# A graph layer on one core: who clears the accumulator, and when the statistics of the raw rows are taken

## The reference

```python
h = relu(layernorm(x))
s, v = h[:, :64], h[:, 64:].reshape(n, 32, 3)
xs = s @ W1_s / sqrt(64);  xv = einsum('nmc,mk->nkc', v, W1_v) / sqrt(32)     # per node: the "table"
w  = silu(edge_embed @ fc_w1 + fc_b1) @ fc_w2 + fc_b2                         # per edge, 192 weights
xs_e, xv_e = xs[src], xv[src]                                                 # gathered by source
m0_a = w_ss * xs_e * sh0;          m1_a = (w_sv * xs_e)[:, :, None] * sh1[:, None, :]
m1_b = w_vs[:, :, None] * xv_e * sh0;  m0_b = w_vv * einsum('emc,ec->em', xv_e, sh1) / sqrt(3)
agg  = segment_sum(concat(m0_a, m0_b, m1_a, m1_b), dst) / sqrt(0.5)
out_s = agg_s @ W2_s / sqrt(96) + s @ Wsc_s / 8
out_v = einsum(agg_v, W2_v) / sqrt(96) + einsum(v, Wsc_v) / sqrt(32)
return x + h + concat(silu(out_s[:, :64]), out_v * silu(out_s[:, 64:96])[:, :, None])
```

## Time and profile before

| | |
|---|---|
| median of 3 runs | 535.98 us (534.12 to 537.64) |
| profiled execution | 534.37 us, its span 532.6 us, 1.8 us around it |
| PE / DVE / ACT / POOL busy | 476.2 / 356.8 / 207.0 / 389.1 us |
| granted TensorE clock, mean | 0.934 of full |
| gathers of the pass (POOL L575) | 382, 364.0 us busy, 121.3 us idle before them |
| chain of waits, share of the span | POOL 34%, PE 21%, issue 20%, DVE 10%, DMA 7% |

### The profile page before, as it was taken

The page is one execution under the profiler, slowest core; times in us unless marked ns, Lnnn a source line. Parts: engine busy times, 40 slices in busy tenths (PEclk is TensorE's granted clock), DMA queues, the critical chain, the costliest instruction groups (busy, mean ns, idle before and its releaser), DMA issues.

```text
span 532.6 us, 18827 instructions
## 1 busy us (share of the span) xinstructions
PE 476.2 (89%) x5423; PEld 352.5 (66%) x5423; DVE 356.8 (67%) x1235; ACT 207.0 (39%) x422; POOL 389.1 (73%) x419
## 2 busy tenths in 40 slices
PE   6965998899988888888998799899999899999995
PEld 6933675767766656666766567577766667766765
DVE  7966975566666666666766666647666676666764
ACT  4834533243434333343343433333344343443421
POOL 7777577777777777777777777777777777777770
PEclk9976999689999999997999989869989999998997
DMA  9943232223332332332223233222223322332320
GB/s 218 275 127 74 49 76 72 70 67 85 75 78 72 76 79 66 82 76 77 72 73 80 67 82 76 74 75 72 75 73 76 77 74 75 79 79 68 82 72 23
DMA packets 35171, 44.15 MB, mean 83 GB/s; under 512 B 10003, under 2 KB 27553, under 8 KB 35113
## 3 DMA queue, kind: packets, MB, share of 16 engines
q0 software_dynamic: 19488, 33.29, 25.1%
q1 hardware_dynamic: 14447, 9.97, 7.2%
q10 hardware_dynamic: 1178, 0.32, 0.3%
HBM read 39.54 MB, written 4.00 MB: 82 GB/s over the span
## 4 chain that ended last, share of the span: by engine, by line
POOL 34%; PE 21%; issue 20%; DVE 10%; DMA 7%; SPq 2%; ACT 2%; ACTq 1%; DVEq 1%; POOLq 0%
POOL gath L575 34%; PE ps L907 7%; DMA gath<-table,src_sb 6%; PE ps L894 3%; PE ps L917 3%; DVE P L721 2%; PE ps L912 2%; DVE agg L396 1%; SPq L529 1%; DVE stats L297 1%; DVE z_sb L315 1%; ACTq L664 1%; ACT aggT L590 1%; DVE agg L761 1%; PE ps L913 1%
## 5 line engine op out<-in xcount | busy, mean ns | idle before, releaser
L575 POOL DMA_INDIRECT gath<-table,src_sb x382 | 364.0, 953 | 121.3 <-issue 110.7
L917 PE MATMUL ps<-S,P 128*64 128x24 f32 x2496 | 168.7, 219 | 0.0
L907 PE MATMUL ps<-fc_sb,hid 128*128 128x384 f32 x416 | 166.1, 525 | 0.5
L917 PEld LDWEIGHTS ps<-S,P 128*64 128x64 f32 x2496 | 157.5, 141 | 0.0
L716 DVE TENSOR_TENSOR P<-ps,gath 128x512 f32<-128x512 f32 x103 | 71.2, 691 | 112.5 <-DMA gath<-table,src_sb 95.4
L912 PE MATMUL ps<-S,P 128*64 128x36 f32 x832 | 118.5, 237 | 28.3 <-DVE P L721 20.1
L912 PEld LDWEIGHTS ps<-S,P 128*64 128x64 f32 x832 | 81.7, 138 | 90.8 <-issue 56.7
L638 ACT COPY ps<-fb_sb 128x768 f32<-128x768 f32 x104 | 83.8, 806 | 92.6 <-DVE P L721 92.6
L761 DVE TENSOR_TENSOR agg<-ps,agg 128x48 f32 x412 | 84.4, 205 | 36.8 <-ACT res L601 8.0
L913 PE MATMUL ps<-S,P 128*64 128x12 f32 x832 | 108.3, 208 | 0.0
L907 PEld LDWEIGHTS ps<-fc_sb,hid 128*128 128x128 f32 x416 | 80.5, 205 | 37.6 <-issue 10.1
(11 more groups left out here) (122 smaller groups left out, 357.7 us busy)
## 6 DMA issues: line engine op xcount, KB each, us to landing
slow<-table SPq DMA_DIRECT2D x773, 0.6 KB
slow<-table ACTq DMA_DIRECT2D x384, 0.6 KB
gath<-table,src_sb POOLq DMA_INDIRECT x382, 2.6
out<-res SPq DMA_DIRECT2D x24, 78.1 KB
x_sb<-x SPq DMA_DIRECT2D x5, 350.0 KB
emb<-emb_t SPq DMA_DIRECT2D x52, 32.0 KB
table<-prod SPq DMA_DIRECT2D x3, 420.0 KB
sh_sb<-sh_t SPq DMA_DIRECT2D x1, 840.0 KB
```

The source lines that it names most:

```text
L575: nc.gpsimd.indirect_dma_start(gath[:, u, j, :], None, table, bass.IndirectOffsetOnAxis(ap=src_sb[:, t:t + 1], axis=0)).then_inc(arrived, 16)
L907: ins = nc.tensor.matmul(w_ps(u)[:, 2 * g:2 * g + 2, 0:WN], hid[:, u % 2, g, :], fc2_sb[:, :, :], start=False, stop=True, skip_group_check ...
L917: ins = nc.tensor.matmul(oj[64:128, :, c:4:3 - c], pj[:, lo:lo + 64], sj[:, :, 0:2 + c:1 + c], start=(c == 0), stop=(c == NC - 1), skip_gr ...
```

## The change

`DVE_CLEAR` goes from 8192 to 5120, so VectorE clears 5120 columns and ScalarE 7428 (before: 8192 and 4356). `HEAD_RAW` goes from 2 to 3: three raw groups are now treated in the head. The moments of group 0 stand between `minima` and `windows`, those of groups 1 and 2 between the output weights and the clear; the scales stay behind the clear. The group left for the pass has its moments behind step 0 of round 1 (before: two groups behind steps 0 and 1 of round 0), its square root at the end of round 1 (before: of round 0), and its scale behind step 0 of round 2 (before: round 1).

```diff
-DVE_CLEAR = 8192
+DVE_CLEAR = 5120
...
-HEAD_RAW = 2
+HEAD_RAW = 3
...
             minima()
+            raw_moments(0)
             windows()
             passes_needed()
             output_weights()
+            for g in range(1, HEAD_RAW):
+                raw_moments(g)
             nc.vector.memset(agg[:, 0:DVE_CLEAR], 0.0).then_inc(s_clear, 1)
-            for g in range(HEAD_RAW):
-                raw_moments(g)
             for g in range(HEAD_RAW):
                 raw_scale(g)
...
                     for i in range(LEAD + 1):
                         for u in range(SLOTS):
                             step(i, u, i - LEAD if i >= LEAD else None)
-                        if i == 0:
+                        if i == 1:
                             for g in range(HEAD_RAW, NR // RG):
                                 raw_std(g)
...
-                            if i == 0 and u < NR // RG - HEAD_RAW:
+                            if i == 1 and u < NR // RG - HEAD_RAW:
                                 raw_moments(HEAD_RAW + u)
-                            if i == 1 and u < NR // RG - HEAD_RAW:
+                            if i == 2 and u < NR // RG - HEAD_RAW:
                                 raw_scale(HEAD_RAW + u)
```

## The result

| | kernel before | changed kernel |
|---|---|---|
| median of 6 runs | 535.06 us (532.47 to 537.64) | 529.65 us (527.55 to 532.19) |
| profiled execution | 534.37 us, span 532.6 | 530.08 us, span 528.4 |

The ratio is 0.9887, 95% interval 0.9853 to 0.9921: 5.4 us faster by the medians, 6.0 by the ratio, 4.2 to 7.9 by its interval. The two profiled executions lie 4.3 us apart.

What follows compares the result with a forecast made beforehand. GpSimd's 382 gathers were taken to bound the kernel, with other engines costing only longer gaps. Removing the 3.87 us stall, all other terms at nothing, gave 535.98 - 3.87 = 532.1 us, range 529.5 to 535.5.

Steps and rivals of the forecast that it cites:

- Moments of group 0: Head, VectorE: 1.95 us of work fits its 2.64 us wait for TensorE and costs nothing.
- The clear: Head, VectorE: clearing 5120 columns takes 5.41 us by scaling the whole stretch, or 6.05 with a fixed hole ahead.
- VectorE's lane: Head: selectors of step 0 end at 43.4 us instead of 46.55, with three scales at 0.24 us each.
- ScalarE's lane: Head: longer clear of 6.51 us, then three square roots; first silu starts at about 37.5 us and ends about 38.
- TensorE's lane: Head: priming until 39.76, then 3.74 us at half clock; first products start at 43.5 us instead of 50.31.
- The gate: GpSimd's wait ahead of step 4: weights of step 2 end by 49.9, before 53.34, so the 3.87 us stall goes.
- Landing in the head: Head: with 3.2 us allowed for a gather to land, the rows of group 2 are there by 27.9 us.
- The group in round 1: Round 1: 1.95 us on VectorE and 2.86 on ScalarE cost nothing, covered by 3.7 us of margin at step 8.
- Rivals 2 and 3: GpSimd stops ahead of step 8 or 10, 537.4 us, chance 0.05; a later gate takes 1 to 3 us, 0.07.
- rival 1: Later in the pass: the two small stalls go too, gain 4.77 us, 531.2 us; chance 0.10.
- Rival 4: Seventeenth gather: something of GpSimd's own holds it after sixteen gathers, so nothing changes, 536 us; chance 0.04.
- the gain in the sum: Whole kernel: only the 3.87 us stall ahead of step 4 is gained, taken from the starting median of 535.98 us.

Runs made afterwards that it cites:

- g2: Changed kernel with one scatter product per tile instead of six and one 128-row transfer per tile for single-row fetches; ratio 0.7237 to the kernel before.
- g3: The kernel of g2 with the clear's shares as before (VectorE 8192, ScalarE 4356 columns); ratio 0.7251 to the kernel before.
- e2 to e4: In order: kernel before with only the clear's shares changed, 0.9999; changed kernel with the old shares, 0.9978; changed kernel with the group in round 0, 0.9964.

## Why the prediction was right or wrong

**The path to the gate was right, the gain was put too small.** I forecast 532.1 us with 0.84 on "within 1%"; it came out 1.1% faster.

- *Moments of group 0* cost nothing, as forecast.
- *The clear* took 5.26 us (34.81 to 40.07) against 5.41 forecast and 6.05 by a fixed hole. The Trainium skill, PSUM — Partial Sum Buffer, in the part on narrow writes, has 1.04 ns per element for a memset of 2-byte elements into PSUM; the trace agrees for these float32 columns of SBUF, as 5.26 us is 1.03 ns a column.
- *VectorE's lane*: selectors done at 43.01, forecast 43.4; the three scales took 0.46 us (40.07 to 40.53) instead of 0.72, which I had taken from rows with a wait between them.
- *ScalarE's lane*: first silu at 36.79, forecast about 37.5.
- *TensorE's lane*: weights of step 0 done at 40.06, forecast 43.5. The priming ended at 38.34 instead of 39.76, and the hidden layer and weights behind it took 1.72 us instead of 3.74. I carried half clock over, but the granted clock was 0.97 from 36 to 37 us and full from there, where before it was 0.50 up to 38 us and again from 44 to 52; TensorE had there been idle from 39.76 to 46.46. Nothing hung on it, as VectorE came last.
- *The gate*: weights of step 2 done at 50.01, forecast 49.9 at the latest; seventeenth gather at 53.52, forecast 53.6. Stall gone, 3.87 us. That 50.01 and 49.9 lie so close is luck: from the first products it took 7.09 us, not the 6.43 that I called the most, as those weights ran at a granted clock of 0.57 (2.60 us against 1.46 before), and the first products came 0.58 us earlier than forecast.
- *Landing in the head*: my bound of 3.2 us was low. The gathers of the raw rows took up to 7.2 us to land in the changed kernel where they started in its first 11 us, while the input was loading, and 3.4 us at most of those from 18 us on whose landing the trace shows. No wait came of it.
- *The group in round 1*: no stall of GpSimd until 167 us. Rivals 2 and 3 have no support, nor has rival 1: two small stalls stand in the pass as before, elsewhere, and cost 1.14 us against 0.90. The table loads took 1.28 us each and the whole detour 2.91 (69.07 to 71.98), against 2.86 forecast; so nothing stands between the loads, the square root and the silu. The Trainium skill, ScalarE: Activation LUTs, What ACT_TABLE_LOAD costs, adds 1.38 us of drain to each switch; these rows don't show it.
- *Rival 4* (GpSimd's own limit) is refuted by the changed kernel itself: with the weights done at 50.01, GpSimd went on behind its sixteenth gather after 0.31 us. Besides, seven kernels start that gather 0.75 to 0.78 us behind the weights of step 2, whatever the gap; that is the delay of an opened gate. The gaps of g2 and g3 at this place have another reason, which is open.

**The step that failed** is the gain in the sum, "535.98 - 3.87". It takes the one stall of one execution as the difference of two medians and puts everything beside it at nothing. That term of 3.87 us measured 5.4 by the medians and 6.0 by the ratio (4.2 to 7.9), so it lies just outside the interval. Of the 5.4 us, 4.3 stand between the two profiled executions: 3.87 at the gate, and some 0.4 in the terms put at nothing (earlier start, shorter gather rows, less a longer tail and longer later gaps). The other 1.1 us come from where these executions lie among the others: that of before is 0.69 us under its median of 535.06, that of after 0.43 above its median of 529.65. The starting point was too high as well: 535.98 was the median of three runs, that of six is 535.06, which makes another 0.9 us of the distance between 532.1 and 529.65.

What the 1.1 us are is open. Each kernel's six runs spread over 5 us, and no trace near 530 us exists of an execution other than the profiled ones. It may be that the profiled execution of before stalled less than others; that is argued, not shown. Nor is there a sign in e2 to e4, which ran at 930 us and more, that the moved group or the clear gives it.

Not shown either is how the gate's stall splits between order and clear near 530 us. An estimate for the order alone: its first products came 3.2 us later than with both (15.2 against 12.0), which would put the end of the weights of step 2 at 50.01 + 3.2 = 53.2. With the 0.77 us of an opened gate the gather would start at 54.0 instead of 53.5. By this the order alone takes away all but some 0.5 us of the stall, and the traces at 930 to 950 us, where it brought the weights of step 2 as early as the whole change, agree in kind.

## What to carry to other kernels

An engine that issues gathers without a pause bounds a kernel even at 73% busy; look for its few long gaps, follow each back to what opened it, and take their sum as what work on other engines can give. It is an estimate and no ceiling on what the medians show: here it was 4.8 us, and they moved by 5.4. Moving short work into a hole that another engine's wait leaves, ahead of a long clear, was free here. Where executions differ by 1%, a stall read from one of them is only one sample, and where the forecast gain (0.7%) is that close to 1%, a gain beyond 1% deserves more than the 0.13 of a tail. Check the starting median too: three runs put it 0.9 us above that of six.

## What the runs showed of the hardware

The same program took 535 us in one session and 932 to 954 us in five others, on five chips. In the changed kernel (528.4 and 931.0 us of span) the gathers took the same time (950 and 951 ns), TensorE's products did not: its weights took 675 ns instead of 532, at a mean granted clock of 0.717 instead of 0.931. Of the 403 us, its busy time accounts for 184 and its idle time for 219. Much of that idle time has nothing in the profile that releases it, above all where TensorE has many short products: 119.8 us ahead of the 2496 products of L918, none at 530 us. Six times fewer scatter products made 952 us into 805, fewer single-row transfers and loads of row numbers besides into 705. What holds the instructions back is open. The memset's row on VectorE leaves out part of its time: 6.88 us for 8192 columns with 1.66 to 1.75 us of apparent idle time ahead of it, 4.33 for 5120 with 1.01 to 1.11.
